# Differential attention on one Trainium2 core: normalising by a reciprocal, and a padded output transpose, in place of cross-multiplied sums and a packed one

## The reference, cut to what matters

```
scores = q @ k^T          # two score matrices for each head, 1024 x 1024, inner size 8
probs  = softmax(scores)  # rows
w      = probs[:, :, 0] - lam * probs[:, :, 1]
attn   = w @ v            # 16 columns for each head
rms    = rsqrt(mean(attn * attn) + 1e-5)
attn   = attn * rms * subln_g * (1 - lambda_init)
```

## Time and profile before

| | |
|---|---|
| median of 3 runs | 6218.06 us (6216.75 to 6225.11) |
| the profiled execution, its own time | 6225.11 us |
| its span | 6223.0 us |
| busy, share of the span | PE 92%, DVE 91%, ACT 76%, POOL 32% |
| granted PE clock, mean over the span | 0.975 |
| DVE row maxima L682 | 4096 instructions, 4782.8 us, mean 1212 ns |
| DVE transpose of sums L694 | 256 instructions, 180.1 us |
| DVE transpose of the output L699 | 128 instructions, 55.7 us |
| POOL power L630 | 128 instructions, 372.5 us |

### The profile page before, as it was taken

How to read it: one execution, slowest core, us unless ns; L and a number is a source line. 1 busy time by engine, 2 the same in 40 slices (tenths; PEclk the granted TensorE clock), 3 DMA queues, 4 the chain that set the end, 5 groups by cost and what they waited for, 6 DMA issues and landing times. The chain is left out here.

```text
span 6223.0 us, 137268 instructions
## 1 busy us (share of the span) xinstructions
PE 5741.3 (92%) x36560; PEld 1767.1 (28%) x36560; DVE 5651.7 (91%) x6200; ACT 4708.3 (76%) x8950; POOL 1998.8 (32%) x3781
## 2 busy tenths in 40 slices
PE   8868999999999999999999999999999999987775
PEld 4541222222222222222222222222222222225423
DVE  7869999999999999999999999999999999966716
ACT  5655888888888888888888888888888888873304
POOL 7971222222222222222222222222222222225406
PEclk9988999999999999999999999999999999998878
DMA  5671222222222222222222222222222222206598
GB/s 179 202 207 35 49 48 48 50 47 48 48 50 50 50 50 50 50 49 49 49 49 49 48 47 47 49 50 50 50 50 50 50 48 50 49 9 199 191 340 276
DMA packets 436713, 491.05 MB, mean 79 GB/s; under 512 B 99283, under 2 KB 298099, under 8 KB 436195
## 3 DMA queue, kind: packets, MB, share of 16 engines
q1 hardware_dynamic: 435171, 483.57, 32.3%
q10 hardware_dynamic: 1024, 0.53, 0.0%
HBM read 360.60 MB, written 123.21 MB: 78 GB/s over the span
## 5 line engine op out<-in xcount | busy, mean ns | idle before, releaser
L682 DVE TENSOR_REDUCE at_largest<-at_ps_m 128x1 f32<-128x1024 f32 x4096 | 4782.8, 1212 | 98.7 <-PE at_ps_m L787 29.1
L668 ACT ACTIVATE at_e<-at_ps_e 128x512 f32<-128x512 f32 x8192 | 4232.0, 603 | 837.5 <-PE at_ps_e L760 837.4
L787 PE MATMUL at_ps_m<-k_stack,q_stack 48*128 48x512 bf16 x8192 | 2749.4, 386 | 119.8 <-DVE at_largest L682 87.6
L760 PE MATMUL at_ps_e<-q_stack,k_stack 51*128 51x512 bf16 x8192 | 2470.5, 382 | 77.7 <-ACT at_e L668 42.2
L775 PE MATMUL at_ps_o<-at_e,at_v 128*32 128x512 f32 x16384 | 2248.8, 620 | 1.1 <-issue 1.1
L760 PEld LDWEIGHTS at_ps_e<-q_stack,k_stack 51*128 51x128 bf16 x8192 | 622.2, 94 | 2472.1 <-ACT at_e L668 2248.3
L587 POOL TENSOR_TENSOR at_negated<-at_zeros,at_largest_t 128x32 f32<-128x32 f32 x256 | 64.3, 251 | 3405.8 <-DVE at_largest_t L689 3405.8
L787 PEld LDWEIGHTS at_ps_m<-k_stack,q_stack 48*128 48x128 bf16 x8192 | 617.5, 93 | 880.8 <-DVE at_largest L682 845.1
L775 PEld LDWEIGHTS at_ps_o<-at_e,at_v 128*32 128x32 f32 x16384 | 452.2, 149 | 502.5 <-issue 354.3
L630 POOL TENSOR_TENSOR at_rms<-at_mean_eps,at_minus_half 128x16 f32<-128x16 f32 x128 | 372.5, 2910 | 10.0
L436 PE MATMUL pr_ps_q<-pr_xn_t,pr_w 128*128 128x512 f32 x512 | 232.6, 597 | 2.5 <-issue 1.8
(11 more groups left out here) (130 smaller groups left out, 2806.3 us busy)
## 6 DMA issues: line engine op xcount, KB each, us to landing
k_stack<-k_parts SPq DMA_DIRECT2D x1536, 64.0 KB
q_stack<-q_parts SPq DMA_DIRECT2D x256, 192.0 KB
q_stack<-q_parts SPq DMA_DIRECT2D x256, 128.0 KB
w_first<-in_w SPq DMA_DIRECT2D x32, 1024.0 KB, 11.7
ex_w_second<-in_w SPq DMA_DIRECT2D x32, 1024.0 KB, 12.8
q_parts<-pr_parts SPq DMA_DIRECT2D x96, 256.0 KB, 2.5
k_parts<-pr_parts SPq DMA_DIRECT2D x96, 256.0 KB, 2.8
pr_x_in<-in_x SPq DMA_DIRECT2D x16, 1024.0 KB, 5.8
```

What stands on the lines that cost most here:

```text
L668: nc.scalar.activation(e[:, j % E_BUFS], ps_e[:, (HALVES * u + j) % SLOTS], ACT.Exp, scale=SCALE).then_inc(exp_done, 1)
L682: nc.vector.reduce_max(largest[:, u % 2, j // SIDE, j % SIDE:j % SIDE + 1], ps_m[:, j % 2], AX.X).then_inc(max_done, 1)
L760: nc.tensor.matmul(ps_e[:, (HALVES * u + j) % SLOTS], k_stack[rows, u, pair, c, kt * P:(kt + 1) * P], q_stack[rows, u, pair, c, half * HAL ...
L787: last = nc.tensor.matmul(ps_m[:, j % 2, half * HALF:(half + 1) * HALF], q_stack[rows, u, pair, c, t * P:(t + 1) * P], k_stack[rows, u, pa ...
```

## The change

Four things are changed in attend, and nothing elsewhere:

1. DVE gets a step `invert` in g = 2: the reciprocal of the 32 sums of a partition (s1 and s2 of 16 blocks), read with a stride of 32 elements out of `sums_t`.
2. POOL's `finish` waits for it, scales the second half of the inverses by -lam, and makes both products in one instruction of 128x512; the four small instructions that made and squared s1 * s2 are gone (15 instructions become 11), and 16 * eps is added as a constant.
3. `attn_t` is 128x512, with 16 filled and 16 zero columns in each block of 32 (zeroed once at the start by POOL), and so DVE's transpose in g = 7 is of 128x512.
4. Each store takes the 16 filled partitions, 2 KB each, in place of 32 partitions of 1 KB.

```diff
-            scaled_s1, both = sb("scaled_s1", [P, BLOCKS]), sb("both", [P, BLOCKS])
-            normed, attn_t = sb("normed", [P, 2, BLOCKS, VD]), sb("attn_t", [P, BLOCKS // 2, 2, VD])
+            inverse = sb("inverse", [P, 2, BLOCKS])
+            normed, attn_t = sb("normed", [P, 2, BLOCKS, VD]), sb("attn_t", [P, BLOCKS, BLK])
...
-            out = sb("out", [P, 2, HALF // 2])
+            out = sb("out", [P, 2, HALF])
...
                     for g in range(QUAD):
                         rows = self.attn_scr[bass.ds(2 * VD * n + VD * (g // 2), VD)]
-                        columns = rows[:, (g % 2) * HALF:(g % 2 + 1) * HALF]
-                        sp.dma_start(columns.rearrange("v (s c) -> s v c", s=2),
-                                     out[32 * g:32 * g + 32, u % 2]).then_inc(out_stored[u % 2], 16)
+                        sp.dma_start(rows[:, (g % 2) * HALF:(g % 2 + 1) * HALF],
+                                     out[32 * g:32 * g + VD, u % 2]).then_inc(out_stored[u % 2], 16)
...
+                nc.gpsimd.memset(attn_t[:], 0.0).then_inc(ones_set, 1)
...
                 def finish(n, base):
-                    s1, s2 = sums_t[:, 0, :, VD], sums_t[:, 1, :, VD]
-                    pool.wait_ge(sums_read, 2 * n + 2 + 1)
-                    nc.gpsimd.tensor_tensor(scaled_s1[:], s1, neg_lam[:].to_broadcast([P, BLOCKS]), ALU.mult).then_inc(
-                        pool_step, 1)
-                    nc.gpsimd.tensor_tensor(both[:], s1, s2, ALU.mult).then_inc(pool_step, 1)
-                    nc.gpsimd.tensor_tensor(normed[:, 0], sums_t[:, 0, :, 0:VD], s2.unsqueeze(2).to_broadcast([P, BLOCKS, VD]),
+                    pool.wait_ge(inverse_done, n + 1)
+                    nc.gpsimd.tensor_tensor(inverse[:, 1], inverse[:, 1], neg_lam[:].to_broadcast([P, BLOCKS]),
                                             ALU.mult).then_inc(pool_step, 1)
                     pool.wait_ge(pool_step, base + 1)
-                    nc.gpsimd.tensor_tensor(normed[:, 1], sums_t[:, 1, :, 0:VD],
-                                            scaled_s1[:].unsqueeze(2).to_broadcast([P, BLOCKS, VD]),
+                    nc.gpsimd.tensor_tensor(normed[:], sums_t[:, :, :, 0:VD],
+                                            inverse[:].unsqueeze(3).to_broadcast([P, 2, BLOCKS, VD]),
                                             ALU.mult).then_inc(pool_step, 1)
                     pool.wait_ge(pool_step, base + 2)
-                    nc.gpsimd.tensor_tensor(both[:], both[:], both[:], ALU.mult).then_inc(pool_step, 1)
...
-                    nc.gpsimd.tensor_tensor(both[:], both[:], sixteen_eps[:], ALU.mult).then_inc(pool_step, 1)
...
-                    nc.gpsimd.tensor_tensor(mean_eps[:], square[:, :, 0], both[:], ALU.add).then_inc(pool_step, 1)
+                    nc.gpsimd.tensor_tensor(mean_eps[:], square[:, :, 0], sixteen_eps[:], ALU.add).then_inc(pool_step, 1)
...
+                def invert(n):
+                    dve.wait_ge(sums_read, 2 * n + 2 + 1)
+                    nc.vector.reciprocal(inverse[:], sums_t[:, :, :, VD]).then_inc(inverse_done, 1)
+
                 def turn_out(n, u):
                     dve.wait_ge(attn_done, n + 1)
                     dve.wait_ge(out_stored[u % 2], 16 * QUAD * ((n + 2 - u % 2) // 2))
-                    nc.vector.transpose(out[:, u % 2], attn_t[:].rearrange("p b s v -> p (b s v)")).then_inc(out_done, 1)
+                    nc.vector.transpose(out[:, u % 2], attn_t[:].rearrange("p b d -> p (b d)")).then_inc(out_done, 1)
...
+                    if g == LAG and last_quad:
+                        invert(n - 1)
```

More of the change, by code:

```diff
@@ L514, in attend @@
                                                             sem("split_done"))
-            max_stored, attn_done, out_done = sem("max_stored"), sem("attn_done"), sem("out_done")
+            max_stored, inverse_done, attn_done, out_done = (sem("max_stored"), sem("inverse_done"), sem("attn_done"),
+                                                             sem("out_done"))
             out_stored, pool_step = [sem("out_stored0"), sem("out_stored1")], sem("pool_step")
-            ONES = 4
-            SPLIT_STEPS, FINISH_STEPS = 4, 14
+            ONES = 5
+            SPLIT_STEPS, FINISH_STEPS = 4, 10
             block = ctx.enter_context(nc.Block())
@@ L598, in finish @@
                 def finish(n, base):
-                    s1, s2 = sums_t[:, 0, :, VD], sums_t[:, 1, :, VD]
-                    pool.wait_ge(sums_read, 2 * n + 2 + 1)
-                    nc.gpsimd.tensor_tensor(scaled_s1[:], s1, neg_lam[:].to_broadcast([P, BLOCKS]), ALU.mult).then_inc(
-                        pool_step, 1)
-                    nc.gpsimd.tensor_tensor(both[:], s1, s2, ALU.mult).then_inc(pool_step, 1)
-                    nc.gpsimd.tensor_tensor(normed[:, 0], sums_t[:, 0, :, 0:VD], s2.unsqueeze(2).to_broadcast([P, BLOCKS, VD]),
+                    pool.wait_ge(inverse_done, n + 1)
+                    nc.gpsimd.tensor_tensor(inverse[:, 1], inverse[:, 1], neg_lam[:].to_broadcast([P, BLOCKS]),
                                             ALU.mult).then_inc(pool_step, 1)
                     pool.wait_ge(pool_step, base + 1)
-                    nc.gpsimd.tensor_tensor(normed[:, 1], sums_t[:, 1, :, 0:VD],
-                                            scaled_s1[:].unsqueeze(2).to_broadcast([P, BLOCKS, VD]),
+                    nc.gpsimd.tensor_tensor(normed[:], sums_t[:, :, :, 0:VD],
+                                            inverse[:].unsqueeze(3).to_broadcast([P, 2, BLOCKS, VD]),
                                             ALU.mult).then_inc(pool_step, 1)
                     pool.wait_ge(pool_step, base + 2)
-                    nc.gpsimd.tensor_tensor(both[:], both[:], both[:], ALU.mult).then_inc(pool_step, 1)
-                    pool.wait_ge(pool_step, base + 4)
                     nc.gpsimd.tensor_tensor(attn[:], normed[:, 0], normed[:, 1], ALU.add).then_inc(pool_step, 1)
-                    pool.wait_ge(pool_step, base + 5)
-                    nc.gpsimd.tensor_tensor(both[:], both[:], sixteen_eps[:], ALU.mult).then_inc(pool_step, 1)
-                    pool.wait_ge(pool_step, base + 6)
+                    pool.wait_ge(pool_step, base + 3)
                     nc.gpsimd.tensor_tensor(square[:], attn[:], attn[:], ALU.mult).then_inc(pool_step, 1)
-                    step = 8
+                    step = 4
                     width = VD // 2
@@ L631, in finish @@
                     pool.wait_ge(pool_step, base + step + 2)
[L632 to L635, removed]
+                    nc.gpsimd.tensor_tensor(attn_t[:, :, 0:VD], attn[:], rms[:].unsqueeze(2).to_broadcast([P, BLOCKS, VD]),
                                             ALU.mult).then_inc(attn_done, 1)
```

## The result

The changed kernel takes 6257.6 us (median of 4, 6254.8 to 6260.9) against 6220.2 us before (6216.8 to 6225.1): ratio 1.0059, 95% interval 1.0042 to 1.0078. That is 37 us more, against 50 foretold, inside the range.

What follows compares the result with a forecast made beforehand. The pace was taken as the loop from a score through its exponential to the next scores and sums, not DVE's; 34 + 18 = 52 us, taken as 50, gave 6268 us against the median of 6218, range 6244 to 6292.

Steps and rivals of the forecast that it cites:

- The pace and the two paid stretches: Attend: 2.425 us a group, set by the score-exponential loop; DVE's extra steps cost 0.55 us a quad, in two places.
- The output transpose: DVE's transpose in attend, 128x512 for 128x256: 0.27 us more a quad, none of it hidden, 34 us in all.
- The new stall: PE in attend: 0.23 us lost in group 8, where nothing was lost before, from the longer output transpose.
- The reciprocal: DVE in attend: 0.37 us long, blocking 0.30, 0.16 forgiven, 0.14 lost a quad; 18 us, between 0 and 48.
- the rival in which the reciprocal is cheap: DVE's reciprocal up to 0.24 us long, its lateness forgiven; 34 us in all, 6252; chance 20%.
- the prediction's two readings: DVE's reciprocal: 8 cycles a column, 8.3 ns, 0.41 us, 22 us; or latency alone, the lower bound.
- POOL too late: If `finish` takes over 11.4 us, DVE waits before its output transpose; 1 us too late is 126 us, 6390; chance 3%.
- Slack hides both: DVE's slack, 0.16 us a group, hides both the transpose and the reciprocal; 6218, no change; chance 5%.
- the faster rival: End of attend's unrolled loop: a hitch of 0.8 us goes, 25 us, with the transpose hidden; 6193; chance 2%.
- the stores with half as many, longer rows and POOL's shorter chain cost nothing: SP, DMA and POOL: same four 32 KB stores a quad cost nothing; POOL's saving is worth nothing.

Runs made afterwards that it cites:

- run 5: Kernel before plus one spare 128x32 DVE reciprocal a quad, its result unused, in group 13: ratio 0.9995.
- run 6: Kernel before plus one spare 128x32 DVE reciprocal a quad, its result unused, in group 8: ratio 1.0035, 22 us.
- run 1: Kernel before with the padded output alone (128x512 transpose, stores of 16 partitions), no reciprocal: ratio 1.0054, 34 us.
- run 8: Changed kernel with its output transpose in group 5 instead of 7, ahead of POOL's result: 6641.6 us, ratio 1.0673.
- run 4: Changed kernel with its output transpose in group 6 instead of 7: ratio to before 1.0031, 19 us over before.
- run 2: Kernel before with the reciprocal and POOL's shorter finish alone, output and stores packed as before: ratio 0.9999.
- run 7: Kernel before plus two spare DVE reciprocals back to back in group 13: ratio 1.0015, 9 us.
- run 3: Kernel before with its output transpose in group 5 instead of 7, nothing else: ratio 0.9983, 10 us faster.

## Why the prediction was right, and where it was off

- **The pace and the two paid stretches** were read rightly: 2.425 us a group, not set by DVE, and DVE's lateness paid behind its group 1 and its groups 7 to 9. Runs 5 and 6 show it on one and the same instruction. That the 2.425 is the loop from a score through its exponential to the next scores was read from PE's waits for ACT; no run changed that loop or PE's own work, so it is not tested.
- **The output transpose**: 0.27 us and fully paid, 34 us. Run 1 measured 34 us, 0.25 to 0.26 a quad. The new stall of 0.23 (in group 9, miscounted as 8) came out to the hundredth.
- **The reciprocal**: 18 us were foretold (0 to 48), some 4 came. The mechanism held, the term was mis-sized. Duration 0.33 and not 0.37; it held DVE for 0.25 (3032.17 to 3032.42) and not 0.30; the two maxima behind it took 1.08 and 1.13 from start to start, not 1.13 each, so that 0.20 was left of it; and with 0.16 forgiven, 0.04 was paid where I had 0.14. Since only the excess over what is forgiven is paid, an error of 0.1 in the lateness, half from the length and half from the quicker maxima, was an error of a factor 3 in the price. The result lies between the rival in which the reciprocal is cheap (6252) and the forecast (6268), nearer to that rival. The rival's condition, a reciprocal of at most 0.24 us, did not hold, though.
- **The Trainium skill on the reciprocal.** The Trainium skill ("VectorE: DVE Perf Modes", section "Walkthrough: the 8-slice pipeline in each mode") says that a reciprocal is an iterative divide with a repeat count of 8; it gives no rate. The reading as 8 cycles a column, 8.3 ns, was the prediction's own. This trace has 331 - 149 = 182 ns for 31 columns more, 5.9 ns each: above the 1.07 ns of a transpose's column, and below 8.3. The measurement decides against the prediction's two readings, 8 cycles a column and latency alone, and not against the sentence.
- **POOL too late** did not happen (3.2 us to spare). Its price had been put at up to 1 us for each us. In run 8, where DVE stood for 1.65 us, a quad grew by 3.2 over run 4; the part beyond the 1.77 that the wait was to cost came with the slow clock.
- **Slack hides both**: refuted for the transpose by run 1, nearly true for the reciprocal by run 2.
- **The loop's end**: untouched, quads with it are 0.79 longer before and 0.80 in the changed kernel and in run 1; the faster rival had nothing.
- **Not settled**: that the stores with half as many, longer rows and POOL's shorter chain cost nothing was not measured by itself. Run 1 holds the stores with the transpose and leaves, at 34 us for 34 worked out, no more than the width of its interval (25 to 42 us) for them. The trace narrows this: a quad grew in groups 4 and 9 to 11 alone, by what DVE's two steps explain.

## What to carry to other kernels

An engine that is 98% busy may still not set the pace; ask of each place what an added step is charged there. Take the step's start-to-start time, subtract the idle time the engine has in that place and what its consumer may be late, and only the rest is paid (a sum made after run 7; it fits runs 3 and 5 too, and the stalls of the first two traces); behind a step that has already used these up, everything is. Before making such a step cheaper, move it away from its neighbours: run 3 won 10 us by moving one instruction two groups, but in the changed kernel the same move by two groups put it in front of its producer (run 8), and cost nearly forty times that.

## What the runs showed of the hardware

- A DVE reciprocal of 128x32 f32 takes 331 ns against 149 for one column (on 64 partitions): 5.9 ns a column, read with a stride of 32 elements. The spare ones, with a stride of 4, took 344 (run 5), 310 (run 6) and 319 ns in the mean (run 7).
- A DVE transpose of 128x512 f32 takes 701 ns out of SBUF and 704 out of PSUM, against 435 for 128x256: 1.04 ns for each further column.
- DVE instructions follow each other before the first has ended: a transpose or reciprocal holds the engine for about 75 to 85 ns less than it lasts (medians of the traces: 701 and 625, 331 and 253, 310 and 228), and the two maxima behind a reciprocal take 2.21 us from start to start, for 2.26 in a row.
- In run 8 a stall of PE of some 1.8 us in two pieces was followed by almost 7 us at half clock in the quad shown, about 4 us a quad over the loop (clock 0.95), while stalls of 0.28 to 0.40 us, three a quad, left the clock at 1.00 in the changed kernel.
